# Two products of the values moved one step later in every batch, and the statistics of four later tiles moved one step earlier in the last batch

## The reference

```
x = x + tanh(g_xattn) * (softmax(rope(ln(x) Wq) rope(ctx Wk)^T / 4) (ctx Wv)) Wout + bout   # 32 heads of 16
h = ln(x);  y = relu(h up)^2 down + (h expert) * (sum of the two largest of h gate)
x = x + tanh(g_ffn) * (layernorm(y) * gamma + beta)
```

## Time and profile before

| | us |
|---|---|
| median of 3 runs | 1585.53 |
| lowest and highest run | 1580.32 and 1586.48 |
| the profiled execution | 1587.19 |
| its span, first to last instruction | 1585.4 |
| PE busy, of the span | 1522.9 (96%) |
| DVE, ACT, POOL busy | 982.8, 632.4, 337.9 |
| mean granted TensorE clock | 0.982 of full speed |
| a batch of the loop (1 to 13), from a step to the same step of the next | 42.92 |
| waits of TensorE for the four FFN tiles of the last batch (steps 5, 8, 11, 14) | 3.44, 0.74, none, 0.79 |
| its waits for an exponential before groups 3 and 4 there | 0.89, 0.69 |

### The profile page before, as it was taken

How to read it: one execution, slowest core, us unless ns; L and a number is a source line. 1 busy time by engine, 2 the same in 40 slices (tenths; PEclk the granted TensorE clock), 3 DMA queues, 4 the chain that set the end, 5 groups by cost and what they waited for, 6 DMA issues and landing times.

```text
span 1585.4 us, 25920 instructions
## 1 busy us (share of the span) xinstructions
PE 1522.9 (96%) x9498; PEld 1127.8 (71%) x9498; DVE 982.8 (62%) x1416; ACT 632.4 (40%) x962; POOL 337.9 (21%) x406
## 2 busy tenths in 40 slices
PE   7789999999999999978999999999999999999997
PEld 6556666666666666545787888878878878788886
DVE  7788888888888888755663535426344364353524
ACT  3265555555556565655442222222222222222221
POOL 5323233233323323211101102102010020110202
PEclk9699999999999999987999999999999999999999
DMA  6645555555565555543430101101010011010101
GB/s 171 141 97 142 132 132 134 129 144 133 130 144 129 126 126 137 121 121 97 140 100 14 47 20 47 34 1 54 27 34 28 20 47 34 14 47 20 54 0 41
DMA packets 80623, 131.11 MB, mean 83 GB/s; under 512 B 21624, under 2 KB 35064, under 8 KB 80504
## 3 DMA queue, kind: packets, MB, share of 16 engines
q1 hardware_dynamic: 80504, 129.48, 31.9%
HBM read 51.17 MB, written 16.78 MB: 43 GB/s over the span
## 4 chain that ended last, share of the span: by engine, by line
PE 84%; DVE 8%; issue 4%; POOL 2%; ACT 1%; DMA 0%; SPq 0%; POOLq 0%; DVEq 0%; ACTq 0%
PE pP L1111 17%; PE pT L1111 11%; PE pA L1312 11%; PE pO L1111 11%; PE pB L1312 11%; PE pO L1237 6%; PE pA L1209 6%; DVE mneg L1532 4%; PE pM L1111 3%; PE pB L1225 3%; PE pP L1118 2%; PE pM L1279 1%; PE pT L1193 1%; PE pM L1118 1%; PE pM L1185 1%
## 5 line engine op out<-in xcount | busy, mean ns | idle before, releaser
L1532 DVE TENSOR_REDUCE mneg<-pA 128x4 f32<-128x1024 f32 x250 | 305.7, 1223 | 111.9 <-PE pA L1209 109.0
L1010 ACT ACTIVATE probs<-pB 128x1024 f32<-128x1024 f32 x249 | 256.1, 1029 | 220.0 <-PE pB L1225 209.9
L1635 DVE TENSOR_TENSOR relu<-relu 128x512 f32<-128x512 f32 x128 | 88.3, 690 | 252.6 <-ACT hid L1064 252.6
L810 POOL TENSOR_SCALAR var_eps<-meanvar 128x1 f32<-128x1 f32 x96 | 34.5, 360 | 965.8 <-DVE meanvar L1414 965.6
L1312 PE MATMUL pA<-dn,hid 128*128 128x512 f32 x768 | 197.1, 392 | 1.7 <-DVE hid L1637 1.5
L1312 PE MATMUL pB<-dn,hid 128*128 128x512 f32 x768 | 195.0, 389 | 0.0
L1111 PE MATMUL pP<-fT,up 128*128 128x512 f32 x768 | 188.5, 394 | 0.0
L1111 PE MATMUL pO<-fT,up 128*128 128x512 f32 x768 | 184.9, 390 | 0.1
L1312 PEld LDWEIGHTS pA<-dn,hid 128*128 128x128 f32 x768 | 142.9, 188 | 34.4 <-DVE hid L1637 5.1
L1111 PEld LDWEIGHTS pO<-fT,up 128*128 128x128 f32 x768 | 143.9, 188 | 30.7 <-issue 0.8
L1312 PEld LDWEIGHTS pB<-dn,hid 128*128 128x128 f32 x768 | 144.2, 188 | 30.0
(11 more groups left out here) (200 smaller groups left out, 1997.3 us busy)
## 6 DMA issues: line engine op xcount, KB each, us to landing
stk<-kT SPq DMA_DIRECT2D x180, 128.0 KB, 2.9
stq<-qT SPq DMA_DIRECT2D x180, 128.0 KB, 3.0
fres<-x_scratch SPq DMA_DIRECT2D x34, 256.0 KB, 2.8
xin<-x SPq DMA_DIRECT2D x32, 256.0 KB, 2.9
numer<-av_s SPq DMA_DIRECT2D x128, 64.0 KB, 2.4
xres<-x SPq DMA_DIRECT2D x32, 256.0 KB, 2.8
x_scratch<-xres SPq DMA_DIRECT2D x32, 256.0 KB, 2.1
out<-y_s SPq DMA_DIRECT2D x32, 256.0 KB, 2.0
```

The lines of the kernel that those rows point to most:

```text
L810: nc.gpsimd.tensor_scalar_add(var_eps[:], meanvar[:, 1:2], EPS).then_inc(ve_made, 1)
L1010: nc.scalar.activation(probs[:, s % 4, :, :, :].rearrange("p a b s -> p a (b s)"), psum[:, :, :], ACT.Exp).then_inc(exp_done, 1)
L1532: nc.vector.tensor_reduce(mneg[par][:, :, 2 * u:2 * u + 2].rearrange("p t q -> p q t"), psum[:, :, :].rearrange("p q (t k) -> p q t k", t= ...
L1635: nc.vector.tensor_tensor(r[:], r[:], r[:], ALU.mult).then_inc(sq_made, 1)
```

## The change

Group 1 of the values' products moves from step 4 to step 5, and group 3 from step 8 to step 9, on TensorE (behind that step's two logits, in front of its jobs) and their copies on ScalarE with them. In the last batch `norm_in` stands two steps before the turn instead of one (steps 3, 6, 9, 12). The first `inv_std` moves in front of `rest_av(14, 0)` in GpSimd's order; the other three stay where they are.

```
+VALUES = {2: 0, 5: 1, 6: 2, 9: 3, 10: 4, 12: 5, 14: 6}
...
-        norm_at = {(i, s - 1): u for (i, s), u in tile_at.items()}
+        norm_at = {(i, s - 2): u for (i, s), u in tile_at.items()}
...                                                    # GpSimd, iteration
+                if isinstance(i, int) and i == B - 1:
+                    inv_std(NT + 1)
                 if within(bt):
                     rest_av(bt, 0)
                 if prepares:
                     rope_sum(b2, "Q0")
                 ending = isinstance(i, int) and i == B - 1
                 if ending:
-                    for u in range(2):
-                        inv_std(NT + u + 1)
+                    inv_std(NT + 2)
...                                                    # ScalarE, iteration
-                    if s % 2 == 0 and s and within(i):
-                        take_av(i, s // 2 - 1)
+                    if s in VALUES and within(i):
+                        take_av(i, VALUES[s])
...                                                    # TensorE, iteration
-                    if s % 2 == 0 and s and within(i):
-                        times_v(i, par % 2, s // 2 - 1)
+                    if s in VALUES and within(i):
+                        times_v(i, par % 2, VALUES[s])
```

## The result

The changed kernel takes **1566.83 us** (median of 4 runs, 1565.3 to 1567.29), the one before 1584.78 (median of 4): a ratio of 0.9887, with a 95% interval of 0.987 to 0.9904. The profiled execution took 1566.75 us (span 1564.9), against 1587.19 (span 1585.4) before.

A forecast was written before the change was run, and what follows sets the result against it. TensorE's order was taken to bound the kernel, so only its idle time could go. Loop -9.2, batch 14 +0.9 and last batch -3.0 gave -11.3 us, from 1585.53 to 1574.2 us; range 1568 to 1582.

The forecast's parts named there:

- the two waits of the loop: Batches 1 to 13, TensorE before the logits of steps 7 and 10: 0.30 and 0.41 us less, 9.2 us in all.
- The rival in which it waits everywhere: Batches 1 to 13: late reciprocals make b1 wait in every batch, slower, 1599 us; chance 0.05.
- the one in which nothing happens: Loop: TensorE's idle time only moves to another step, only the last batch's change counts, 1583 to 1585; chance 0.03.
- Half of it: Batches 1 to 13: one of the two waits comes back because a margin was too small, 1578.7 us; chance 0.13.
- the first tile's turn: Last batch: the first FFN tile's turn comes at 712.55 instead of 715.40, 2.85 us earlier.
- the wait that I named as a bound: Last batch: third tile's `inv_std` waits on GpSimd behind `rest_av(14, 1)`, costing the second tile's gain; 1 us more at worst.
- the term +0.9: Batch 14: b1 stays put, savings are waited away, group 3 behind it runs at half clock; 0.9 us more, between 0 and 4.
- the last batch, -3.0: Last batch: b1 2.5 us earlier, group 3 at half clock costs 1.84, waits of 2.2 go; 3 us less.
- 2.2 - 1.84 = 0.36: Last batch: waits before the second and fourth tile and of group 4, 2.2 us, go; group 3 behind b1 costs 1.84.
- 6 less, if the clock never falls: Last batch: bound on the gain if TensorE stays at full clock, 6 us less.
- No half clock in the last batch: Last batch: half clock absent, 15.2 us less in all, 1570 us; chance 0.12.
- Clock at the end: Batch 14 and last batch: longer waits before b1 prolong half clock, +4 and +1 us, 1581 us in all; chance 0.17.

The follow-up runs named there:

- group 3 put back: Changed kernel with group 3 of the values' products back at step 8, in front of b1, in batches 14 and 15 only: 1568.22 us, 0.99.
- the values alone: Kernel before with groups 1 and 3 of the values' products one step later, statistics and GpSimd's order as before: 1571.85 us, 0.9922.
- the statistics alone: Changed kernel with groups 1 and 3 back at steps 4 and 8, keeping the earlier statistics and GpSimd's new order: 1579.76 us, 0.9969.
- the run with both edits: Changed kernel, reciprocals' DMAs ahead of the residual's, 6 constant transposes before b1 in batch 14, 12 before step 8's logits in the last batch: 1563.55 us, 0.9874.

## Why the prediction came out as it did

**Right: the two waits of the loop.** Both go, each by its own edit (group 3 alone, group 1 alone). Forecast were 0.30 and 0.41 us, measured 0.37 to 0.38 and 0.47. The order of what is late next holds too: at step 7 a wait under 0.2 us stays (414.31 + 0.99 = 415.30, the logits at 415.47), at step 10 K1's rotation sets kT1. The 0.14 that was missing is 0.06 from the four transposes in front of step 6's logits, which take 0.53 us (413.11 to 413.64) instead of the 0.59 I had left in, 0.06 from kT1, 0.56 instead of 0.62 (423.55 to 424.11), and the rest rounding. Over 13 batches it is 1.7 us (10.87 against 9.2). b1 doesn't wait in the middle batches: it starts at 421.35, with no bracket, between K and the logits of step 9. The rival in which it waits everywhere is out, and so is the one in which nothing happens. *Half of it* shows once: one of the 13 batches is 0.15 us longer than the others. In it K1's product starts 0.81 us behind step 7's logits instead of 0.67, where this rival saw the margin; the trace shows no wait there, so that this is the reason isn't shown.

**Right: the first tile's turn.** It comes 5.06 us after the start of group 0's products (692.58 to 697.64) instead of 7.98 (707.42 to 715.40), 2.92 less; the working had 2.85. GpSimd's wait is the ordinary 1.13, as said. The third tile's `inv_std` has the wait that I named as a bound, 2.93 us, and TensorE doesn't wait for that tile. The reciprocals' last issue falls back by 0.27 us (forecast 0.3). b1 starts 3.61 us earlier, a little more than the 1.65 to 3.35 that I gave.

**Wrong: batch 14, the term +0.9.** The step that failed is "b1 stays where SP puts it, what steps 4 and 8 save is waited away in front of b1, and group 3 behind it costs". It took the 3.9 us from issue to b1 as fixed. It is not: it was 2.16 after, 2.10 in another execution of the kernel before, and 3.57 with group 3 put back. Nor did the half clock grow: from 10.2 us it went to 6.8, and to 10.2 in a second execution of the changed kernel. The wait in front of b1 stayed at 1.96 us (0.67 in the second execution), where I had 4. Of the -3.24 in the two profiles, 1.75 is this landing, 0.22 SP's chain, and 1.27 the work behind b1, where the half clock lasted 3.4 us less. In medians it is less: the values alone gained 12.3, of which 10.9 are the loop. The other 1.4 are batch 0, batch 14 and what the groups do in the last batch together, **about 1 us less where 0.9 more was forecast**. With an uncertainty of 2 us the medians alone don't settle the sign; the batch's own length in the profiles (40.2 to 42.0 us in the old order but for the one at 35.73, 37.7 to 38.9 after) speaks for less.

**Wrong in size: the last batch, -3.0.** b1 to the FFN's first product took 1.64 us less, where the sum had 2.2 - 1.84 = 0.36. I had kept the stretch at half clock whole and charged group 3 on top. It shrank from 17.1 to 6.8 us. It goes mostly with the wait for the first turn: in the ten profiles in which the first turn waited 1.9 to 3.4 us, half clock took 10.2 to 17.1 us of the last batch (17.1 in five, 13.7 in three, 10.2 in two, in one stretch or two, and with the values alone the first began before that wait), in the eight in which it waited 0.5 us 6.8 to 10.2 (10.2 in two: the statistics alone and group 3 back; in three others 3.4 more follow at 740 us, as the FFN begins). Of the forecast's two bounds the one below, "6 less, if the clock never falls", was the nearer. In medians this part gives 4.4 alone, and 5.7 on top of the values alone.

**The sum**, in medians: 10.9 (loop) + 1.4 (the rest of what the values alone gained, by the profiles mostly batch 14) + 4.4 (statistics and GpSimd's order, last batch) = 16.7, and 1.3 by which both together do better, 18.0. The forecast had 9.2 - 0.9 + 3.0 = 11.3. Of the 6.7 between, 1.7 is the loop, 2.3 batch 14 with what comes under the same 1.4, 1.4 the last batch and 1.3 what the parts do together; all but the first are no surer than the 2 us of the ratios. The rival *No half clock in the last batch* was nearest in number and in kind, though the half clock was shortened and not gone. *Clock at the end*, with 0.17, pointed the wrong way: both the forecast and this rival took a longer wait in front of b1 for granted.

The Trainium skill ("TensorE: Matmul & The Clock Gate", section "HAM oscillation — how this bites in real kernels") was read as a reason that nothing can be gained in batch 14. The runs agree only in part. In the last batch every profile has at least 6.8 us at half clock, and more where TensorE waited longer for the first turn. But in batch 14 the same program had 10.2 us of it in one execution and none in another, and the clock fell behind waits of 0.33 and 1.08 us as well.

**Open.** What decides in one execution of the same kernel whether batch 14 runs at full clock isn't settled. Transposes in b1's wait went with full clock after the change and not before it, and a later instruction packet didn't bring full clock either. How much of the term +0.9 was wrong by the landing and how much by the clock is therefore known for the two profiles only. That the packet itself delays the reciprocals is likely from the table, with one profile against it, but only its place was moved, never the packet taken away. Why both parts together gain 1.3 us more than their sum was not traced; it is within the uncertainty of the three ratios.

## What to carry to other kernels

Where one engine's order sets the time, list its waits in a batch and move a piece of work from in front of each into the gap: two moves of 0.99 us of products, without one instruction less, took 0.85 of 42.92 us. Look after that at what a repaired wait does to the clock, since the first turn, 2.9 us earlier, brought 4.4 us in a run of its own. And take a landing time or a half-clock stretch that a single trace shows at the end of a phase for one draw of a spread, and look at a second execution of the kernel before, if there is one, before a term is built on it.

## What the runs showed of the hardware that was not expected

- In batch 14 a 16 KB DMA of the reciprocals landed in 1.8 to 2.2 us when the next 16 KB packet of the queue "q8 instruction" came 3.3 us or more behind its issue, and in 3.5 to 3.8 us in five of six profiles where it came 1.3 to 1.7 us behind (2.0 in the sixth). Twelve transposes fewer in the opening, 600 us earlier, moved that packet 2.5 us; twelve more didn't.
- The clock fell to half behind a row of waits of about 1 us (0.33 and 1.08 in the run with both edits), and in another execution of the kernel before it stayed full through batch 14. With a landing that was 1.8 us shorter there, that made 5.2 us of difference in one batch.
- An edit of the order of two products changed how fast a DMA came in: with group 3 back ahead of b1 the landing was 3.48 us instead of 2.06, and the wait in front of b1 2.53 us, though b1 stood later in TensorE's order.
